# The written-out orders of five engines in a state-space scan with attention

## What is computed

```
xr, gate = split(x @ W_in.T); xr += style
xc = silu(causal_conv_of_4_taps(xr) + b_conv)
xn = layernorm(xc) * ln_g + ln_b
B, C, dt = split(xn @ W_xproj.T)                  # 16 numbers each
Ad = 1 - tanh(dt @ W_dt.T + b_dt) * 0.01 * tanh(A_log)
Bd = B * min(norm(xn), 1)
h  = clip(h * Ad + Bd * xn, -10, 10)              # 64 tokens in a row; h is 16 x 512
y  = C . h + D * xn
x  = x + (y * silu(gate)) @ W_out.T
z  = normalised(x * s1); q, k, v = z @ Wq.T, z @ Wk.T, (z @ Wv.T) * s2, each scaled
x  = x + softmax(q k.T / 4) v @ Ww.T * dcoef_w + v @ Wu.T * dcoef_u
```

## Time and profile before

| | |
|---|---|
| time of the profiled execution | 1813.53 us |
| its span, first to last instruction | 1811.8 us |
| median of the three runs | 1810.15 us |
| TensorE matmuls (PE) busy | 1594.8 us, 88% |
| TensorE weight loads (PEld) busy | 1036.9 us, 57% |
| VectorE (DVE) busy | 1402.2 us, 77% |
| ScalarE (ACT) busy | 1136.2 us, 63% |
| GpSimd (POOL) busy | 1196.3 us, 66% |
| mean granted TensorE clock | 0.946 of full speed |

### The profile page before, as it was taken

The page is one execution under the profiler, slowest core; times in us unless marked ns, Lnnn a source line. Parts: engine busy times, 40 slices in busy tenths (PEclk is TensorE's granted clock), DMA queues, the critical chain, the costliest instruction groups (busy, mean ns, idle before and its releaser), DMA issues. The chain is left out here.

```text
span 1811.8 us, 41467 instructions
## 1 busy us (share of the span) xinstructions
PE 1594.8 (88%) x12460; PEld 1036.9 (57%) x12460; DVE 1402.2 (77%) x2354; ACT 1136.2 (63%) x2913; POOL 1196.3 (66%) x1849
## 2 busy tenths in 40 slices
PE   5438688999999999999999999999899999989886
PEld 5423245666656565656665665656566665546664
DVE  1758677888878888888888788888888888778542
ACT  5664455767667676767676666667676666333552
POOL 0576577787777778777877777777777778323231
PEclk8667789999999999999999999999999999999997
DMA  4135565465555556655665655665556656445220
GB/s 105 45 89 116 113 144 134 121 141 143 130 140 140 133 145 148 148 136 128 140 143 129 142 136 135 145 152 134 140 126 138 150 131 153 114 112 125 66 65 24
DMA packets 223116, 226.37 MB, mean 125 GB/s; under 512 B 53488, under 2 KB 179056, under 8 KB 222896
## 3 DMA queue, kind: packets, MB, share of 16 engines
q1 hardware_dynamic: 222896, 223.71, 51.8%
HBM read 152.45 MB, written 71.17 MB: 123 GB/s over the span
## 5 line engine op out<-in xcount | busy, mean ns | idle before, releaser
L1704 DVE CUSTOM_DVE_ANT_0 gc<-ps_u,gc,hi 128x512 f32<-128x512 f32 x1008 | 812.0, 806 | 75.0 <-issue 2.2
L985 PE MATMUL ps_y<-gc,cms 128*32 128x512 f32 x2048 | 286.4, 632 | 0.3 <-DVE gc L1704 0.2
L970 PE MATMUL ps_u<-xs_sb,stage 64*128 64x512 bf16 x1024 | 201.2, 435 | 69.8 <-issue 51.5
L1286 ACT ACTIVATE a_tap<-a_xr,conv_w 128x128 f32<-128x128 f32 x768 | 244.2, 398 | 8.6 <-DVE a_xr L1636 8.6
L1303 ACT ACTIVATE a_z<-ps,a_nb,a_rs 128x512 f32<-128x512 f32 x64 | 49.7, 777 | 183.1 <-POOL a_nb L583 183.1
L1051 PEld LDWEIGHTS ps<-c_zT,L1T 128*128 128x128 f32 x1024 | 121.2, 194 | 70.9 <-issue 70.6
L550 POOL TENSOR_TENSOR a_tap<-a_tap 128x512 f32<-128x512 f32 x116 | 147.7, 1275 | 16.1 <-ACT a_tap L1286 16.1
L970 PEld LDWEIGHTS ps_u<-xs_sb,stage 64*128 64x128 bf16 x1024 | 76.7, 186 | 137.0 <-issue 92.7
L1051 PE MATMUL ps<-c_zT,L1T 128*128 128x128 f32 x1024 | 130.7, 281 | 24.3 <-DVE c_o L1788 21.0
L923 PE MATMUL ps<-a_xT,WinT 128*128 128x128 f32 x1024 | 139.3, 294 | 10.4 <-ACT a_xT L1276 9.4
L923 PEld LDWEIGHTS ps<-a_xT,WinT 128*128 128x128 f32 x1024 | 133.2, 210 | 16.5 <-ACT a_xT L1276 10.1
(11 more groups left out here) (180 smaller groups left out, 3555.3 us busy)
## 6 DMA issues: line engine op xcount, KB each, us to landing
xs_sb<-xn_parts SPq DMA_DIRECT2D x256, 192.0 KB
xn_parts<-a_parts SPq DMA_DIRECT2D x128, 192.0 KB, 3.0
skip_d_xn<-a_dx SPq DMA_DIRECT2D x64, 256.0 KB, 2.2
xs_sb<-xn_parts SPq DMA_DIRECT2D x128, 128.0 KB
scan_out<-y_sb SPq DMA_DIRECT2D x256, 64.0 KB
c_dx<-skip_d_xn SPq DMA_DIRECT2D x64, 256.0 KB, 6.0
c_y<-scan_out SPq DMA_DIRECT2D x64, 256.0 KB, 5.5
c_wu<-style_rows SPq DMA_DIRECT2D x128, 128.0 KB, 4.3
```

Source lines behind the costliest of these rows:

```text
L970: pe.matmul(ps_u[r][t % 2][:, :], weights[:, :, l * SPAN + 2 * t + r], xs_sb[rows, sig % 2, t, :], start=True, stop=True).then_inc(s[f"b_u ...
L985: pe.matmul(ps_y[quad:quad + 32, :], cms[:, sig % 2, v, r, 32 * u:32 * (u + 1)], gc[r][:, (2 * u + v) % RING, :], start=(u == 0), stop=(u ...
L1286: ins = act.activation(a_tap[:, tap, m, :].rearrange("p (r t) -> p r t", r=2), a_xr[:, m, :, tap:tap + S], ACT.Identity, bias=bias, scale= ...
L1704: dve._custom_dve(bass.dve_ops.TENSOR_ADD_SAT, out=gc[r][:, t % RING, :], in0=ps_u[r][t % 2][:, :], in1=before, s0=hi[:, c % 4, col:col + ...
```

## The change

The lists of `second_step`, `step` and `late_step` are written anew on GpSimd, TensorE, ScalarE and VectorE, with other banks where calls moved. The same functions are called with the same tiles, so no instruction is added or taken away. On SyncE `load_w` moves behind `load_dx` and `load_y`. `first_step`, `last_step` and everything outside the lists stay.

```diff
@@ SyncE, step @@
                 if chain_due(i, 1) is not None:
                     store_b(chain_due(i, 1))
-                    load_w(chain_due(i, 1))
                 load_dx(c0 + 1)
                 load_y(c0 + 1)
+                if chain_due(i, 1) is not None:
+                    load_w(chain_due(i, 1))
                 load_wu(c0 - 2)
                 store_bct(i - 3)
                 store_dx(i - 2)
...
@@ TensorE, step, as it is now @@
+                a_project_bc(i - 3, 2)
+                a_transpose_x(i, 1)
+                c_weigh_v(c0 - 3, 0)
+                c_transpose_z(c0 - 2, 1)
+                scan_block(sig, 0)
+                c_transpose_o(c0 - 3, 2)
+                c_transpose_x(c0, 1)
+                c_project_k(c0 - 2, 0)
+                a_transpose_xc(i - 2, 2)
+                c_project_wu(c0 - 3, 1)
+                c_project_qv(c0 - 2, 0)
+                scan_block(sig, 1)
...
@@ ScalarE, step, its end as it is now @@
+                c_exp(c0 - 2, 1)
+                c_exp(c0 - 2, 0)
+                c_take_ygT(c0, bank[2])
+                c_take_pT(c0 - 2, 1, bank[1])
+                c_block_values(c0 - 2, bank[0])
+                a_first_part(i - 2)
+                a_take_bcT(i - 3, bank[1])
+                c_take_pT(c0 - 2, 0, bank[0])
+                a_take_tap(i, 2)
+                a_tanh(i - 1)
+                c_normalise(c0 - 1)
+                a_square_sum(i - 2)
```

More of the change, by code:

```diff
@@ L781, in step @@
                 spread_c(sig)
-                a_second_rest(i - 3)
-                c_bias(c0 - 1)
                 a_var(i - 2)
+                if chain_due(i, 1) is not None:
+                    split_b(chain_due(i, 1))
                 a_root(i - 2)
                 a_bias(i - 2)
-                if chain_due(i, 1) is not None:
-                    split_b(chain_due(i, 1))
+                a_half(i - 1, 1)
+                a_offset(i - 2)
+                a_gain(i - 2)
+                a_shift(i - 2)
                 c_sum_skip(c0)
                 c_gate_product(c0)
-                a_gain(i - 2)
-                a_shift(i - 2)
+                c_join(c0 - 3)
+                a_second_rest(i - 3)
                 a_scale_b(i - 3)
-                a_offset(i - 2)
+                c_bias(c0 - 1)
                 a_half(i - 1, 0)
+                a_sum(i - 1)
+                c_style(c0)
+                c_final(c0 - 3)
+                a_norm_root(i - 2)
                 a_skip(i - 2)
[L797 to L801, removed]
                 c_var(c0)
-                c_final(c0 - 3)
                 a_first_rest(i - 2)
@@ L1459, in second_step @@
                 sig = i - SCAN_LAG
-                b_take_y(sig - 1)
[L1461 to L1465, removed]
+                a_take_tap(i - 1, 1)
+                a_take_tap(i - 1, 0)
+                a_take_xT(i, bank[0])
+                a_second_part(i - 3)
+                a_take_tap(i - 1, 3)
+                b_take_y(sig - 1)
                 a_normalise(i - 2, bank[0])
+                a_take_bcT(i - 3, bank[2])
@@ L1814, in second_step @@
                 sig = i - SCAN_LAG
+                if chain_due(i, 1) is not None:
+                    prepare(chain_due(i, 1))
                 a_silu(i - 2)
+                a_bound_norm(i - 3)
                 scan_step(sig, 0, 0)
@@ L1819, in second_step @@
                 scan_step(sig, 1, 1)
-                a_bound_norm(i - 3)
-                if chain_due(i, 1) is not None:
-                    prepare(chain_due(i, 1))
+                a_stats(i - 2, bank[0])
+                a_take_bc(i - 3, bank[2])
+                a_mean_var(i - 2)
                 scan_step(sig, 2, 0)
@@ L1833, in second_step @@
                 scan_step(sig, 5, 1)
-                a_add_style(i, bank[2])
+                a_add_style(i, bank[1])
                 scan_step(sig, 6, 0)
```

180 lines of the change are left out of this document (77 added, 103 removed).

## The result

The changed kernel took 1838.1 us (median of four runs, 1831.54 to 1838.38) against 1810.88 us for the kernel before (four runs, 1808.18 to 1816.89): a ratio of 1.0137, 95% interval 1.0103 to 1.0171. The change makes the kernel slower by about 25 us. I had forecast 1824, slower; the time lies in the range.

The account below looks back on a forecast made before the run. TensorE bounds plain steps, SyncE's queue chain steps. Twelve chains +19, start of full steps +1.5, second_step -1, last chain -6: +13.5 on 1813.5 is 1827, as median (3.4 lower) 1824 us; range 1790 to 1848.

Parts of the forecast that it names:

- The mechanism: SyncE's queue in a chain step: store_dx waits for a_dx, done 1.2 us after the first scan, with raw's load behind.
- B's parts: SyncE's store of B's parts in a chain step: issued 14.3 us after the first scan, against 11.52 before.
- From the parts to the scan: Way from issuing B's parts to the new chain's first scan: 5.92 + 9.55 us as before, plus 0.3 for two loads.
- The chain step: The step holding the way into a new chain, set by SyncE: from 27.0 to 29.7 us, plus 0.3 for loads.
- VectorE's wait: In the chain step, VectorE waits 3.5 to 4 us at the early prepare for raw, hidden behind SyncE.
- Rival A: Faster: SyncE not held by a_dx, raw issued 3.4 us before the first scan, chain step 24.8, total 1756; 14%.
- twelve chains: Chains of four steps: each +2.7 - 3 x 0.48 + 0.3 = +1.6 us, together +19.
- The plain step: Step without a way into a new chain: the wait for c_o goes, 0.3 us for a_xT comes; 23.5 us, gain 0.48.
- Rival C: Clearly slower: TensorE waits for c_yg, c_ygT or c_q, plain steps stay at 23.98; 1840 to 1846 us; 18%.
- The wait for the weights: TensorE's wait in the chain step before the new chain's first L970: grows from 2.3 to 4 us.
- The start: Beginning of the run: chain at the start of the full steps +1.5 us, second_step -1.
- The last chain: No a_dx in its steps, prepare and split_b first: B's parts some 6 us sooner, TensorE's wait shrinks, -6 us.

Follow-up runs that it names:

- the fastest kernel: Changed kernel with store_dx last on SyncE, a_dx ahead of c_style, store_b ahead of store_y, split_b ahead of a_var: 1745.33 us, ratio 0.9606.

## Why the prediction was right, and where it was off

The mechanism held in the chain step at each point that it named. One of them came out as close as it did by luck.

- **`a_dx`.** Forecast 1.2 us after the first scan, from the lengths of the earlier trace rows; measured 1.24. Before, it was done 7.24 ahead of it. SyncE waits for it in 63 of its 64 steps. That the figure is so exact is luck: in the step shown VectorE's last subtraction ends at 1186.25, so from there to `a_dx` it took 11.57 us (forecast 10.7), and to the first scan 10.29 (forecast 9.5). Both were 0.8 to 0.9 too short, and the difference came out.
- **B's parts.** Forecast at 14.3; measured 14.34, 2.6 later than before (forecast 2.7).
- **From the parts to the scan.** 6.22 + 9.41 us against 5.95 + 9.27, 0.4 more, where I took 0.3. The run with the weights first shows that their place is not the reason: its sum is 15.73.
- **The chain step.** Forecast 29.7, with 0.3 for the loads; measured 29.98. Behind it 24.45, 0.73 above a plain step (forecast 0.7).
- **VectorE's wait.** Forecast 3.5 to 4 us; measured 3.58, and hidden, as the run with the late `prepare` shows.
- **Rival A** (SyncE not held, 1756) did not come, and its time was too low for its condition: with `a_dx` or the store out of the way the ratios are 0.979 and 0.981, that is 35 to 38 us faster than before and not the 54 forecast, with chain steps of 25.5 to 25.8 where I had 24.8.
- **The skill's rule.** The Trainium skill, DMA: Bandwidth & Descriptors, section Issuing engines are not separate DMA queues, calls the sequencer's issue time usually small against the DMA itself. Twelve issues add up here: after the change, too, SyncE issues without a pause from 1204.40 to the parts at 1210.73, while they have been ready since 1207.16. With the four issues of `store_y` (2.8 us) behind the parts these went out at 7.39 and not at 10.4 to 10.7. (The moved `store_y` alone has no run.) The 60 us of `store_dx` are something else, a wait ahead of other issues, and say nothing on that sentence.

All three terms of the sum were mis-sized, and they partly cancel. By the traces the change is +21.9, the forecast +13.5.

| | forecast | measured in the traces |
|---|---|---|
| start, to the first scan of chain 2 (counted from 0) | +0.5 | 309.8 - 306.1 = +3.7 |
| twelve chains | 12 x 1.6 = +19 | 1222.4 - 1195.8 = +26.6, 2.2 each |
| last chain | -6 | 92.5 - 101.1 = -8.6 |
| sum | +13.5 | +21.7 |

**The plain step** was what was mis-sized in the twelve chains: 23.5 forecast, 23.72 measured. The new wait was right: I had 0.3 us before `c_transpose_z` for `a_xT`, and TensorE's idle time in a plain step is (569.30 - 562.48) / 24 = 0.28, all of it there. What I had wrong was that TensorE's own 23.24 us would stay: it is busy 23.44. (The step in the earlier trace rows is cut 1 us ahead of the first scan at 952.51; the mean of the 24 plain steps is 23.98 us with 23.23 busy, so nothing hangs on that.) Between the start of one group and the next, less the waits, the gate went from 1.73 to 1.91 us and the input projection from 1.88 to 2.02. Before, each read-out was followed by transpositions or by a wait. Other groups became shorter, but by less in all. Three steps of four times 0.2 make the 0.6 by which a chain missed. I had kept the groups' lengths from the old order, and they change with the order. Rival C had the size (plain steps near 23.98) from another cause, a new wait, and that did not come.

**The wait for the weights**, no term of the sum, was to grow to 4 us. It is 1.46 in the step shown: TensorE had lost its time sooner in the same step, 2.4 us waiting for `gc` (0.57, 1.36 and 0.48) and 1.7 in the gate at the lower clock. The end of the step did not move, since SyncE sets it.

**The start.** From chain 1 to chain 2 the first full steps have few `c_` calls yet. Two of them took 22.54 and 21.33 us before; they take 23.58 and 23.78 now. I had credited each with a gain of 0.48. Up to their start the changed kernel is 1.4 us ahead (234.00 against 235.41; forecast 1), and the chain step behind them takes 28.45 us against 26.79, so the start is -1.4 + 1.0 + 2.4 + 1.7. The rows:

```profile
235.41:257.95 22.54, 19.01 (x93) 10.29 (x97) 16.58 (x27) 11.39 (x31) 16.13 (x23) 0.85 0.73 160
257.95:279.28 21.33, 18.02 (x103) 9.54 (x99) 16.48 (x27) 11.65 (x31) 17.01 (x26) 0.92 0.51 122
```

```profile
234.00:257.58 23.58, 20.45 (x103) 9.76 (x106) 16.58 (x27) 11.08 (x29) 15.48 (x21) 0.83 0.51 125
257.58:281.36 23.78, 18.90 (x99) 8.93 (x91) 17.34 (x28) 11.94 (x31) 16.66 (x26) 0.86 0.55 123
```

TensorE is busy for 18 to 20 us of these steps in either kernel, so the waits between engines take part in setting them. Which wait it is in the new order no run took apart.

**The last chain.** TensorE's wait of 7.24 us before its first scan shrank to 1.16 us, by 6.1, as forecast, since B's parts went out 7.41 us after the step's first scan and not 14.18. But the chain step as a whole went from 30.84 to 21.73 us, 9.1 less, and the three steps ahead of it were 0.5 longer. The traces divide the 9.1: B's parts go out 6.8 sooner, the weights 5.57 us behind them against 6.41, and the first scan comes 8.75 us behind the weights against 10.25. Why these last two became shorter no run took apart.

## What to carry to other kernels

Where one engine issues all DMAs in order, read its list as one more engine's: the store that waits longest sets the start of every transfer behind it, even if nobody needs that store soon. Put first what a later step waits for, and last what nobody does; this one place was worth about 60 us, and the new orders of four engines, without it, 38 (1778.59 against 1816.85). When a list is laid out with the lengths of an old trace, take the length of a group with what stands ahead of it, and lay out the ends of the program apart.

## What the runs showed of the hardware that I had not expected

- A group of TensorE matmuls right behind the 32-column read-outs takes longer: with a transposition in between, which costs 0.165 us, the gate gets 0.10 us shorter and the input projection 0.22. Right behind a read-out a group's first weight load starts with its first matmul and not 0.11 us ahead of it, and that matmul takes 0.10 us longer.
- In the step shown TensorE waited 2.4 us for `gc` between 1203 and 1206.4, and from 1207.83 to 1211.25 the granted clock stood at the lower level (1.2 of 2.4 GHz). The gate then took 3.68 us in place of 1.99. In the chain steps it was low for 4.65 us after the change, for 0.30 before, and for 0.02 in the fastest kernel; in the steps behind them for 1.04, 1.91 and 0.27. With 5.43 us of it, in the run with the late `prepare`, the chain step was as long (30.10), and with none of it 28.96: SyncE set its end.
- GpSimd's `c_ve`, 128x1, took 0.19 us in all 64 steps of the kernel before. Behind `a_dx` it took about 0.64 in 41 of the 64, as in the chain step shown:

```profile
1197.78 0.64 POOL L718 TENSOR_TENSOR c_ve<-c_mv,eps 128x1 f32<-128x1 f32 x1
1198.37 0.19 POOL L719 TENSOR_TENSOR c_nmu<-c_mv,neg_one 128x1 f32<-128x1 f32 x1
```

It lay on no path that sets the end, and no run took it apart.
